# Routing and linear-memory stages of a ViT tower: turned rows of h instead of turned normalised rows, shorter routing chains, grouped output

## The reference

```python
h = _L0_tok_ref(x, ...)                       # patches, layernorm, linear
h = h + _L0_attn_ref(_layernorm(h), ...)      # quantised attention, 12 heads
h = h + _L0_ffn_ref(_layernorm(h), ...)       # 4 experts, best one per row
h = h + _L1_attn_ref(_layernorm(h), ...)      # linear memory
h = h + _L1_ffn_ref(_layernorm(h), ...)       # 8 experts, best two per row
```

```python
q = (x @ w_query.T); k0, v0, g0 = k[0], v[0], gate[0]
retrieved = q_t @ fw;  fw = 0.95 * fw + 0.1 * g0_t * outer(k0_t, v0_t)   # for t in 0..15
return x + retrieved @ w_out.T                # x is the normalised input
```

## Time and profile before

| | |
|---|---|
| median of 3 runs | 668.74 us (664.69 to 669.52) |
| the profiled execution | 671.4 us |
| its span in the trace | 669.6 us |
| PE busy | 494.1 us (74%) |
| DVE busy | 350.9 us (52%) |
| ACT busy | 184.1 us (27%) |

### The profile page before, as it was taken

The page is one execution under the profiler, slowest core; times in us unless marked ns, Lnnn a source line. Parts: engine busy times, 40 slices in busy tenths (PEclk is TensorE's granted clock), DMA queues, the critical chain, the costliest instruction groups (busy, mean ns, idle before and its releaser), DMA issues.

```text
span 669.6 us, 12936 instructions
## 1 busy us (share of the span) xinstructions
PE 494.1 (74%) x4594; PEld 447.5 (67%) x4595; DVE 350.9 (52%) x1072; ACT 184.1 (27%) x396; POOL 143.3 (21%) x146
## 2 busy tenths in 40 slices
PE   4999998866243336499999168733799999999960
PEld 3999994556132333489999166513699999999960
DVE  1677997458998894422221567758122222222206
ACT  3620125225983042032443040300021122122110
POOL 1590000000001000434421100000444444444220
PEclk9999999957566657699999788765799999999995
DMA  8970000000003001495569300201866556656216
GB/s 314 410 266 9 1 1 0 2 4 1 0 15 152 0 22 73 125 261 159 161 188 366 114 1 0 95 0 32 227 187 206 176 171 194 193 156 198 75 61 245
DMA packets 35236, 81.43 MB, mean 122 GB/s; under 512 B 6870, under 2 KB 17970, under 8 KB 34034
## 3 DMA queue, kind: packets, MB, share of 16 engines
q1 hardware_dynamic: 29618, 69.36, 31.8%
q0 software_dynamic: 5568, 11.41, 6.0%
HBM read 70.33 MB, written 10.42 MB: 121 GB/s over the span
## 4 chain that ended last, share of the span: by engine, by line
PE 62%; DVE 22%; issue 5%; ACT 4%; DMA 4%; SPq 1%; another core or an unknown queue 1%; POOL 0%; ACTq 0%; DVEq 0%; POOLq 0%
PE ps L1029 17%; PE ps L1005 12%; PE ps L769 11%; PE ps L1013 6%; DVE stat L1167 2%; PE ps L884 2%; PE ps L853 2%; PE ps L854 2%; PE ps L749 1%; PE ps L970 1%; DMA arena<-tok_w 1%; DMA xn<-made 1%; DVE xT L1629 1%; DVE h L1759 1%; PE ps L751 1%
## 5 line engine op out<-in xcount | busy, mean ns | idle before, releaser
L1029 PE MATMUL ps<-arena,xn 128*128 x696 | 123.2, 328 | 4.2 <-ACT xn L681 1.9
L1029 PEld LDWEIGHTS ps<-arena,xn 128*128 128x128 f32 x696 | 111.8, 190 | 6.6 <-issue 6.3
L447 POOL DMA_INDIRECT xT<-rows,from_i x58 | 56.0, 966 | 220.6 <-DVE to_i L1663 165.9
L769 PE MATMUL ps<-arena 128*128 128x192 f32 (+1 forms) x588 | 86.2, 337 | 10.1 <-DMA arena<-x_strips 9.9
L1005 PE MATMUL ps<-xn,arena 128*128 128x128 f32 x696 | 91.3, 283 | 1.3 <-DVE xn L1673 1.3
L769 PEld LDWEIGHTS ps<-arena 128*128 128x128 f32 (+1 forms) x588 | 84.1, 197 | 10.8 <-issue 10.0
L1005 PEld LDWEIGHTS ps<-xn,arena 128*128 128x128 f32 x696 | 89.3, 200 | 1.7 <-issue 1.4
L1671 DVE COPY xn<-ps 128x128 f32<-128x128 f32 x58 | 16.9, 292 | 124.8 <-PE ps L997 102.0
L459 POOL DMA_INDIRECT made<-xT,to_i x58 | 57.0, 983 | 110.6 <-DVE xT L1683 66.5
L684 ACT ACTIVATE xn<-ps 128x384 f32<-128x384 f32 x78 | 32.6, 493 | 126.0 <-PE ps L1015 99.9
L1013 PE MATMUL ps<-xn,arena 64*128 64x128 f32 x348 | 44.1, 278 | 0.0
(11 more groups left out here) (350 smaller groups left out, 758.2 us busy)
## 6 DMA issues: line engine op xcount, KB each, us to landing
arena<-ffn_a SPq DMA_DIRECT2D x58, 384.0 KB
arena<-ffn_b SPq DMA_DIRECT2D x116, 96.0 KB
arena<-x_blocks SPq DMA_DIRECT2D x16, 384.0 KB, 6.5
arena<-x_strips SPq DMA_DIRECT2D x3, 1536.0 KB, 12.3
arena<-ffn SPq DMA_DIRECT2D x4, 1152.0 KB
rows<-xn SPq DMA_DIRECT2D x8, 384.0 KB, 2.5
xn<-made SPq DMA_DIRECT2D x8, 384.0 KB, 4.0
arena<-tok_w SPq DMA_DIRECT2D x8, 288.0 KB, 6.8
```

Source lines behind the costliest of these rows:

```text
L447: pool.indirect_dma_start(sx[:, k % 6], None, F["src"], bass.IndirectOffsetOnAxis(from_i[:, k:k + 1], 0)).then_inc(sem(f"sx_in{k % 6}"), 16)
L769: mm = pe.matmul(sum_ps(name, j), xs[rows, strip, 2 * j + b, 128 * c:128 * c + 128], w[rows], start=(name, j // 2) not in opened, stop=lef ...
L1029: mm = pe.matmul(ps[:, result_bank(k, N), 0:DIM], hT[:, u % 2, 128 * c:128 * c + 128], F["w2"][:, bass.ds(e2 + DIM * c, DIM)], start=(c == ...
```

## The change

- The routers and the linear stage turn `h` itself (`turn_rows`), not `xn`, as soon as a group of four tokens is final. The normalisation is put in afterwards: the gate weights get their column means subtracted once (`gate_neg`, products by the identity during attention), so the mean of a row drops out, and the logits are multiplied by the row's inverse deviation on DVE.
- Turned rows stay token-major and contiguous. ACT alone copies them. Logits are made with 128 turned rows held in the array and the 4 or 8 gate columns passing (`logits`), so they need not be turned back.
- All of `xn` is written by ACT (`all_norms`), only for `rows_out`. The linear stage's residual h + xn is written as one scaled copy, eight tokens on ACT and eight on DVE (`plus_normed`).
- Keys, values and gates of the linear stage are made for the 16 tokens of image 0 only (`first0`, `first1`), which DVE normalises first. The 16 output products, the turning of h and the second router's logits are interleaved on PE.
- `choose` writes its one-hot directly in bf16; the softmax leaves the chain (only the two chosen logits are used, and `pk` is worked out last). The counting products take bf16. `hot` is made before `place`, its second half by ACT (`hot_rows`), and the product that inverts the slots starts with the first four `place` columns. `from_i` comes before `te_i`, and POOL starts on `from_i` alone. `place` carries the number of the column as a factor.
- Both choices of a row are adjacent rows of `made`. The end is worked in four groups: read, add, store.

```diff
+                made = F["made"][0:F["sel"] * TOKS, :].rearrange("(b r) c -> b r c", b=IMGS)
+                for i in range(4):
+                    r = slice(4 * F["sel"] * i, 4 * F["sel"] * (i + 1))
+                    sp.dma_start(got[n][:, r, :], made[:, r, :]).then_inc(sem(f"back_{i}"), 16)
...
+            for i in range(4):
+                sp.wait_ge(sem("h_final"), i + 1)
+                sp.dma_start(out[:, 4 * i:4 * i + 4, :], h[:, 4 * i:4 * i + 4, :]).then_inc(sem("out_done"), 16)
+            sp.wait_ge(sem("out_done"), 64)
...
+                pool.wait_ge(sem("places"), 2 * n + 1)
...
+                pool.wait_ge(sem("places"), 2 * n + 2)
...
+            def all_norms(n):
...
+                act.wait_ge(sem("near_xn"), 5 + 2 * n)
...
+                    for t in range(4 * i, 4 * i + 4):
+                        ins = act.activation(xn[:, t, :], h[:, t, :], ACT.Identity, bias=stat[:, 480 + t:481 + t], scale=stat[:, 464 + t:465 + t])
+                    ins.then_inc(sem("xn_act"), 1)
...
+                    act.activation(xT0[:, 512 * i:512 * i + 512], ps[:, bank, :], ACT.Copy).then_inc(sem("xT0_ready"), 1)
+                    act.activation(xT1_half(stage, i), ps[0:K1, bank + 1, :], ACT.Copy).then_inc(sem("xT1_ready"), 1)
...
+            def hot_rows(F):
+
+                hot = in_tile(F)
+                act.wait_ge(sem("hot"), F["n"] + 1)
+                act.activation(hot[:, :, 1, :], hot[:, :, 0, :], ACT.Copy, scale=cst[:, C_P:C_P + 1]).then_inc(sem("hot_rows"), 1)
...
+            all_norms(0)
+            hot_rows(F0)
...
+            for t in range(NTOK // 2):
+                ins = act.activation(h[:, t, :], h[:, t, :], ACT.Identity, bias=stat[:, 480 + t:481 + t], scale=stat[:, 448 + t:449 + t])
+            ins.then_inc(sem("h_plus"), 1)
...
+            act.activation(d16, d16, ACT.Exp).then_inc(sem("soft_exp"), 1)
+            all_norms(1)
+            hot_rows(F1)
...
+            def turn_rows(stage, i, ready):
+
+                pe.wait_ge(sem("h_row"), ready)
+                if i >= 2:
+                    pe.wait_ge(sem("xT0_ready"), 4 * stage + i - 1)
+                    pe.wait_ge(sem("xT1_ready"), 4 * stage + i - 1)
+                bank = turn_bank(stage, i)
+                for j in range(4):
+                    pe.transpose(ps[:, bank, 128 * j:128 * j + 128], h[:, 4 * i + j, 0:128], ident)
+                for j in range(4):
+                    mm = pe.transpose(ps[0:K1, bank + 1, 128 * j:128 * j + 128], h[:, 4 * i + j, 128:DIM], ident)
+                mm.then_inc(sem("xT_ps"), 1)
...
+            def logits(F, i):
...
+                for t in range(4 * i, 4 * i + 4):
+                    cols = slice(128 * t, 128 * t + 128)
+                    pe.matmul(lg[:, t, :], xT0[:, cols], gate_w0[n][:], start=True, stop=False, skip_group_check=True)
+                    mm = pe.matmul(lg[:, t, :], xT1[:, cols], gate_w1[n][:], start=False, stop=True, skip_group_check=True)
+                if i == 3:
...
-                oh = rt[:, 512:512 + cols]
-                pe.matmul(ps[:, 5, 0:cols], cst[:, C_TRI:C_TRI + 128], oh, start=True, stop=True)
-                pe.matmul(ps[:, 6, 0:cols], ones, oh, start=True, stop=True).then_inc(sem("rank_ps"), 1)
+                pe.matmul(ps[:, 6, 0:cols], ones_bf[:], one_hot(F), start=True, stop=True)
+                pe.matmul(ps[:, 5, 0:cols], below_bf[:], one_hot(F), start=True, stop=True).then_inc(sem("rank_ps"), 1)
...
+                pe.wait_ge(sem("hot_rows"), n + 1)
                 for c in range(16 * F["sel"]):
+                    if c % 4 == 0:
+                        pe.wait_ge(sem("placed"), 4 * n + c // 4 + 1)
...
-                keep_clock(26 if n else 20, 3)
+                keep_clock(16 if n else 20, 3)
...
+            pe.wait_ge(sem("scalars"), 3)
+            keep_clock(18)
+            turn_rows(1, 0, 1)
+            turn_rows(1, 1, 1)
+            logits(F0, 0)
+            logits(F0, 1)
+            turn_rows(1, 2, 2)
+            turn_rows(1, 3, 2)
+            logits(F0, 2)
+            logits(F0, 3)
...
-            keep_clock(18)
+            last = TILES0 - 1
+            pe.wait_ge(sem(f"y_st0{last % 3}"), 16 * (last // 3 + 1))
+            keep_clock(16)
             for i in range(4):
-                transposes(2, i)
+                turn_rows(2, i, 3 + i)
+            keep_clock(48)
+            pe.wait_ge(sem("near_xn"), 6)
+            pe.matmul(ps[:, 6, 384:416], ones[0:1, :], stat[0:1, 464:496], start=True, stop=True).then_inc(sem("first_ps"), 1)
             pe.wait_ge(sem("xT0_ready"), 12)
...
-                    o = ps[:, bank, 128 * c:128 * c + 128]
-                    pe.matmul(o, w0[:, 128 * c:128 * c + 128], xT0[:, 0:128], start=True, stop=False)
-                    mm = pe.matmul(o, w1[:, 128 * c:128 * c + 128], xT1[:, 0:128], start=False, stop=True)
+                    o = ps[:, bank, 128 * c:128 * c + NTOK]
+                    pe.matmul(o, w0[:, 128 * c:128 * c + 128], first0, start=True, stop=False)
+                    mm = pe.matmul(o, w1[:, 128 * c:128 * c + 128], first1, start=False, stop=True)
...
+            def out_products(i):
+
+                pe.wait_ge(sem("lin_p"), i + 1)
+                for t in range(4 * i, 4 * i + 4):
+                    if t >= 6 and t % 2 == 0:
+                        pe.wait_ge(sem("h_row"), 6 + t // 2 - 2)
+                    mm = pe.matmul(lin_ps(t), PT[:, 128 * t:128 * t + 128], Bo, start=True, stop=True)
+                    if t % 2:
+                        mm.then_inc(sem("lin_o"), 1)
...
+            out_products(0)
+            out_products(1)
+            turn_rows(3, 0, 8)
+            out_products(2)
...
-            pt = PT.rearrange("p (b t) -> p b t", t=NTOK)
...
+            turn_rows(3, 1, 10)
+            logits(F1, 0)
+            out_products(3)
+            turn_rows(3, 2, 12)
+            logits(F1, 1)
+            turn_rows(3, 3, 14)
+            logits(F1, 2)
+            logits(F1, 3)
...
+                dve.tensor_scalar(stat[:, 448:464], y, 1.0, None, ALU.add)
...
-                        ins = dve.tensor_scalar(xn[:, t, :], h[:, t, :], mv[:, t, 0:1], y[:, t:t + 1], ALU.subtract, ALU.mult)
-                    ins.then_inc(sem("xn_ready"), 1)
...
-                link(dve.scalar_tensor_tensor(ge, iota, 8.0, idx.unsqueeze(2).to_broadcast([128, NTOK, E]), ALU.subtract, ALU.is_equal))
-                link(dve.tensor_copy(oh.rearrange("p e t -> p t e"), ge))
+                return dve.scalar_tensor_tensor(oh, iota, 8.0, idx.unsqueeze(2).to_broadcast([128, NTOK, E]),
+                                                ALU.subtract, ALU.is_equal)
...
+                link(dve.tensor_tensor(lg, lg_of(n, E), stat[:, 464:480].unsqueeze(2).to_broadcast([128, NTOK, E]), ALU.mult))
...
+                    link(dve.tensor_tensor(lg, lg, gate_b[:].unsqueeze(1).to_broadcast([128, NTOK, E]), ALU.add))
+                    ins = choose(oh[:, 0], lg, a16, ge, b16, E)
...
+                    link(choose(oh[:, 0], lg, a16, ge, b16, E))
+                    link(dve.scalar_tensor_tensor(lg, oh[:, 0], -1e30, lg, ALU.mult, ALU.add))
+                    ins = choose(oh[:, 1], lg, c16, ge, b16, E)
+                ins.then_inc(sem("chosen"), 1)
+                if n:
+                    dve.tensor_tensor(d16, c16, a16, ALU.subtract).then_inc(sem("soft_in"), 1)
                 dve.wait_ge(sem("rank_ps"), n + 1)
-                tot = rt[:, 768:768 + cols]
+                tot, sums = rt[:, 768:768 + cols], ps[:, 6, 0:cols]
...
-                link(dve.tensor_copy(tot, ps[:, 6, 0:cols]))
-                link(dve.tensor_tensor_scan(inc, cst[:, F["seg"]:F["seg"] + cols], tot, 0.0, ALU.mult, ALU.add))
+                link(dve.tensor_tensor_scan(inc, cst[:, F["seg"]:F["seg"] + cols], sums, 0.0, ALU.mult, ALU.add))
...
-                link(dve.tensor_tensor(hot[:, :, 0, :], cst[:, C_TILE:C_TILE + N].unsqueeze(1).to_broadcast(wide),
-                                       tile.unsqueeze(2).to_broadcast(wide), ALU.is_equal))
-                link(dve.tensor_tensor(hot[:, :, 1, :], hot[:, :, 0, :],
-                                       cst[:, C_TILE + 1:C_TILE + 1 + per].unsqueeze(2).to_broadcast(wide), ALU.mult))
-                dve.tensor_scalar(hot[:, :, 0, :], hot[:, :, 0, :], cst[:, C_P:C_P + 1], None, ALU.mult).then_inc(sem("hot"), 1)
+                dve.tensor_tensor(hot[:, :, 0, :], cst[:, C_TILE:C_TILE + N].unsqueeze(1).to_broadcast(wide),
+                                  tile.unsqueeze(2).to_broadcast(wide), ALU.is_equal).then_inc(sem("hot"), 1)
+                for c in range(per):
+                    ins = dve.tensor_scalar(place[:, c, :], iota_bf[:], spot[:, c:c + 1], float(c + 1), ALU.is_equal, ALU.mult)
+                    if c % 4 == 3:
+                        ins.then_inc(sem("placed"), 1)
...
+                dve.wait_ge(sem("inverse_ps"), n + 1)
```

(36 more changed lines are left out.)

297 lines of the change are left out of this document (127 added, 170 removed).

## The result

The changed kernel takes 639.35 us (median of 4 runs, 636.34 to 641.38) against 669.13 us (4 runs, 664.69 to 670.08) for the kernel before: the ratio is 0.9556 with an interval of 0.9525 to 0.9587. That is 29.8 us or 4.4% faster. The forecast was 628.5 us and a range of 620 to 639, so the time lies 0.35 us above the range, and 10.9 us above the forecast. The direction was right, the size too large.

A forecast was written before the change was run, and what follows sets the result against it. Outside the expert loops, a chain of small DVE and PE handoffs was taken to bound the kernel. Gains 14 + 27.5 + 1.7 - 3 = 40.2 us took the profiled execution from 671.4 to 631.2, median 628.5 us, range 620 to 639.

The forecast's parts named there:

- Clock: Key and logit products: parts fall to 1.2 GHz because short products do not hold PE's clock; 3 us subtracted.
- Rival 2: Uncovered PE stretches in routers and linear stage: a third to half runs cold, 12 us lost, 637.5 us; chance 0.18.
- First router: Layer 0, normalising chain to expert loop: shorter chain starts the experts earlier, 14 us gained.
- the two bounds: Layer 0 expert start: first gather 14.7 us earlier, first weights 12.7 us earlier; the gain lies between.
- rival 1: Expert loop starts: loops begin when weights come, only 12.7 and 23.8 count, 35.2 in all, 633.5 us; chance 0.15.
- Linear stage and second router: Between the expert loops: first gather 27.7 us earlier, first weights 23.8; 27.5 us gained over both parts.
- Gates' preparation in attention: Attention: added gate products, copies, casts and broadcasts hide in waits for DVE, costed at nothing; at worst 2 us.
- End: Final additions and stores: first group waits about 1 us more, last store is a quarter; 1.7 us gained.
- rival 4: Expert loops: scatters into adjacent rows land much later and hold PE; at 2 us a tile 706 us; chance 0.01.
- rival 5: Both routers: ACT's xn rows come late and hold the gathers, gain halves, 649 us; chance 0.02.
- How the profiled execution stands to the median: Whole kernel: median of runs lies 2.7 us below the profiled execution, so 631.2 becomes 628.5 us.
- Rival 3: Whole kernel: clock kept, experts start warm, gains of 14.7 and 28.5, 624 us; chance 0.10 for below 622.

The follow-up runs named there:

- widened ones: Changed kernel with key, value and gate products passing 128 columns (636.25 us), and changed kernel with logit products passing 128 columns (638.96 us).
- after again: The changed kernel once more, unaltered, on the third chip: 640.03 us, ratio 0.9578 to the kernel before.
- one store: Changed kernel with one store of the whole output behind the last addition instead of four behind each group: 643.17 us, ratio 0.9603.
- more filler: Changed kernel with 56 filler products ahead of the keys instead of 48: 640.96 us, ratio 0.9538.
- weights first: Changed kernel with te_i made ahead of place in both routers, so the first weights are issued earlier: 640.26 us, ratio 0.9544.
- wide keys and logits: Changed kernel with key, value, gate and logit products all passing 128 columns, second run, beside the unaltered changed kernel: 632.48 us, ratio 0.9464.
- the kernel before with narrow keys: Kernel before with its 36 key, value and gate products passing 16 columns instead of 128: 674.16 us, ratio 1.005.
- the run of both edits: Changed kernel with key, value, gate and logit products all passing 128 columns, first run: 632.89 us, ratio 0.9414.

## Why the prediction was wrong

**The step that failed** is the term "Clock. Short products do not hold PE's clock up [...] I subtract 3 us". It was sized too small, and its reason was half right: the row behind it has short products that alternate with waiting, and rival 2 was held down because "filler products stand ahead of each part". The clock fell while PE never stopped. In the traces it cost 3.2 us in the first logits, 3.7 from key to S, 2.3 from S to the outputs and 2.2 in the last stretch (changed kernel against the widened ones), 11.4 us in this execution: 8.4 of the 9.0 us that are missing in it. In four other profiles with narrow keys and logits (after again, one store, more filler, weights first) these four stretches lost 5.8 to 10.8.

In the time it is less. On the chip that ran both, wide keys and logits took 7.6 us off the changed kernel, so the term was 4.6 us too small, of the 10.9 by which the median missed the forecast. The kernel with wide products takes 632.5 us, where the forecast without its clock term would be 625.5. Of these 7 us the first router's term explains about 2.5 (below); the rest stays open. Rival 2 gave 637.5 us, which was the profiled execution, and missed the median by 1.9. Its 12 us fit the stretches of this execution, and are more than the 7.6 of the time; that it came so near the median is in part luck, since it leaves the first router at 14 us, which measured less.

What misled me was the earlier trace rows: "The linear stage ran at 1.00". I took that as a property of a stage in which PE is kept busy. It was a property of keys that pass 128 columns, and the change takes exactly these columns away. The Trainium skill ("TensorE: Matmul & The Clock Gate", HAM oscillation — how this bites in real kernels) tells of a clock that falls when PE waits, and asks for no long idle gaps. In the changed kernel PE was busy 10.14 of 10.14 us and its clock was at 0.57; that section does not cover this case.

The other steps, each without the 2.7 us of the unchanged input stage:

- *First router* (14 us forecast, 8.3 measured at the additions behind loop 0; 11.5 with the clock's 3.2 given back). The chains were right: choosing to gather gained 2.1 where I had 2.2, and `xn` was stored from 247.1 and never waited for. With the clock's 3.2 given back the gather came 14.3 us earlier and the weights 12.6, as the two bounds said (14.7 and 12.7). But I took 14 between them, and the weights were last (rival 1): the first down-product came 9.3 us earlier, as the weights (9.4), not as the gather (11.1). A further 1.0 us went between there and the additions. The loop itself did not grow: from the first down-product to the last scatter it is 79.0 us, and 79.2 before. From that scatter to the additions it took 6.6 us instead of 5.5 (6.3 to 8.4 in the other runs with the changed kernel's code). The four reads of `made` were issued over 3.22 us instead of 1.76 and landed after 4.7 us instead of 4.0 (medians); why is not shown.
- *Linear stage and second router* (27.5 forecast, 21.2 measured to the first down-product, 29.4 with the clock's 8.2 given back). Keys came 1.5 us behind the statistics' end, as forecast. "With 16 columns nothing is gained if the load sets the pace" was right: 0.22 us a product with either width. Choosing to gather took 19.6 where I had 18.6.
- *Gates' preparation in attention*, at nothing: the last scale of attention comes at 230.7 and 230.9 us in two profiles without it and at 228.1 to 232.0 in eleven with it. It stayed hidden.
- *End*: adding began 1.1 us later, where the read-back of twice the bytes was forecast to cost 1, and the tail gave 2.7: 1.7 net, as forecast.
- *Slower by scattering* (rival 4) and *late `xn`* (rival 5): neither happened. The last `xn` store of router 0 was issued by 252.7 (247.14 + 5.58) and such a store lands in 2.3 us, 6.6 us ahead of the first gather.
- *How the profiled execution stands to the median*: I subtracted 2.7 us, since before was profiled in a long execution. The changed kernel was profiled in a short one, 1.9 below its median. Between the medians the two kernels differ by 29.8 us.
- *Rival 3* adds up 14.7 and 28.5; for the 28.5 the prediction has no source, its largest gain from linear stage and router being the 27.7 of the first gather.

## What to carry to other kernels

When a change narrows what passes through TensorE, price the clock as well as the columns: where a product took 0.22 us with 16 columns and with 128, fewer passing columns saved nothing, and they halved the clock for them and for part of what followed, here at a price of 7.6 us in the time (5.8 to 11.4 in the stretches of five profiles). Repeating the columns by a broadcast cost nothing there and gave it back. Where an expert loop begins with weights and gathered rows at once, find out for each loop which comes last; here it was the weights in one and the rows in the other, and the version that issues the weights early in the first alone has the lowest time.

## What was not expected of the hardware

- TensorE fell from full to half clock without a pause: at 382.13 us of the changed kernel, 1.3 us into products of 128 rows held and 16 columns passed, and at 399.24 of the kernel before with narrow keys, 1.8 us into them. With the same instructions, the same wait ahead of them and 128 columns, in the kernel before, it did not.
- At full clock f32 products with 16 columns and with 128 start at the same spacing, 0.22 us. At half clock it is 0.43 with 16 (382.13, 382.55, 382.98 in the changed kernel) and with 128 (384.77, 385.20 in the run of both edits).
- What the narrow products lose differs between executions: 11.4 and 8.1 us in two profiles of the changed kernel, and 5.8 to 10.8 in three of its variants that keep them. On one chip the changed kernel's times spread over 7.5 us (635.88 to 643.4) and those of the widened one over 3.9 (630.32 to 634.19).
